# Spaced indirect transfers, a second product one step later and four buffers in a mixture-of-experts kernel

## The reference, cut to what matters

```python
x = x + 0.5 * ffn(layernorm(x))
x = x + attention(layernorm(x))      # causal, one head, within each of the 4 sequences
x = x + 0.5 * ffn(layernorm(x))

def ffn(x):                          # 8 experts, w1 128x512, w2 512x128
    probs = softmax(x @ router_w.T)
    topv, topi = top_k(probs, 2);  topv = topv / (topv.sum() + 1e-9)
    y = sum over the two chosen experts e of  topv_e * (gelu(x @ w1[e]) @ w2[e])
```

## Time and profile before

| what | value |
|---|---|
| median of 3 runs without the profiler | 332.69 us (332.57 to 332.88) |
| the profiled execution, its span | 421.0 us |
| granted TensorE clock, mean of the span | 0.850 |
| PE busy | 273.8 us |
| PE weight loads | 249.7 us |
| DVE busy | 152.5 us |
| ACT busy | 139.4 us |
| POOL busy | 140.6 us |
| indirect transfers issued by POOL | 135 |

### The profile page before, as it was taken

The page is one execution under the profiler, slowest core; times in us unless marked ns, Lnnn a source line. Parts: engine busy times, 40 slices in busy tenths (PEclk is TensorE's granted clock), DMA queues, the critical chain, the costliest instruction groups (busy, mean ns, idle before and its releaser), DMA issues.

```text
span 421.0 us, 7028 instructions
## 1 busy us (share of the span) xinstructions
PE 273.8 (65%) x1957; PEld 249.7 (59%) x1958; DVE 152.5 (36%) x687; ACT 139.4 (33%) x267; POOL 140.6 (33%) x159
## 2 busy tenths in 40 slices
PE   0505193499981599985356853699709999596930
PEld 0404183399981599963246531698709998595930
DVE  3583331222210067312497632556102222132234
ACT  1101231255540345542131412265205564243420
POOL 9047257200047200047200373000770005666550
PEclk9999996699995599998595985789866999798785
DMA  7971112522222112111000011011221222222115
GB/s 218 411 199 51 62 58 63 200 64 69 70 76 68 44 56 64 37 45 50 25 1 2 19 50 56 9 37 51 77 67 46 70 65 69 62 63 71 55 55 164
DMA packets 38520, 31.79 MB, mean 76 GB/s; under 512 B 5224, under 2 KB 34416, under 8 KB 38112
## 3 DMA queue, kind: packets, MB, share of 16 engines
q1 hardware_dynamic: 33744, 18.12, 15.2%
q0 software_dynamic: 4752, 13.40, 9.2%
HBM read 15.68 MB, written 15.81 MB: 75 GB/s over the span
## 4 chain that ended last, share of the span: by engine, by line
PE 52%; another core or an unknown queue 15%; DVE 12%; issue 11%; POOL 5%; ACT 3%; DMA 2%; DVEq 0%; POOLq 0%; ACTq 0%; SPq 0%
PE bank L890 20%; PE bank L879 19%; POOL slots_in L395 3%; PE bank L870 3%; DVE xs L707 2%; PE bank L832 2%; PE bank L847 2%; PE bank L939 2%; DVE stats L565 1%; PE bank L901 1%; DMA y_rows<-final_rows 1%; DVE xs L740 1%; DVE neg_max L731 1%; PE bank L902 1%
## 5 line engine op out<-in xcount | busy, mean ns | idle before, releaser
L890 PE MATMUL bank<-w_sb,act 128*128 x736 | 106.4, 291 | 49.5 <-issue 25.4
L890 PEld LDWEIGHTS bank<-w_sb,act 128*128 128x128 f32 x736 | 97.1, 206 | 52.0 <-issue 51.9
L879 PE MATMUL bank<-xT,w_block 128*128 128x128 f32 x736 | 108.3, 295 | 0.1
L879 PEld LDWEIGHTS bank<-xT,w_block 128*128 128x128 f32 x736 | 99.7, 210 | 0.9 <-issue 0.5
L468 ACT ACTIVATE act<-bank 128x512 f32<-128x512 f32 x92 | 54.9, 597 | 133.8 <-PE bank L879 68.9
L693 DVE COPY yb<-bank 128x128 f32<-128x128 f32 x92 | 26.7, 291 | 178.7 <-PE bank L890 109.7
L407 POOL DMA_INDIRECT y_rows<-slots_out,slot_of x48 | 46.0, 957 | 101.5 <-DMA slots_out<-yb 87.5
L462 ACT COPY w_block<-w_sb 128x512 f32 x92 | 56.4, 614 | 20.0 <-issue 20.0
L395 POOL DMA_INDIRECT slots_in<-xn,slot_of x32 | 30.9, 966 | 58.9 <-DVE slot_of L641 49.7
L418 POOL DMA_INDIRECT final_rows<-yb,row_of x23 | 22.8, 989 | 51.5 <-DVE row_of L683 38.7
L870 PE MATMUL bank<-ident,xb_numbered 128*128 128x128 f32 x92 | 28.2, 307 | 17.9 <-DMA xb_numbered<-slots_in 10.5
(11 more groups left out here) (104 smaller groups left out, 221.1 us busy)
## 6 DMA issues: line engine op xcount, KB each, us to landing
xb_numbered<-slots_in SPq DMA_DIRECT2D x69, 64.0 KB
slots_out<-yb SPq DMA_DIRECT2D x69, 64.0 KB
w_sb<-in_L_ffn_w SPq DMA_DIRECT2D x8, 512.0 KB, 8.1
slots_in<-zeros POOLq DMA_DIRECT2D x2, 1472.0 KB, 12.0
numbered_slots<-numbered POOLq DMA_DIRECT2D x1, 1483.5 KB, 5.5
xb_numbered<-numbered_slots SPq DMA_DIRECT2D x23, 64.5 KB
xs<-in_L_attn_x SPq DMA_DIRECT2D x4, 256.0 KB, 3.5
out<-xs SPq DMA_DIRECT2D x8, 128.0 KB
```

The lines of the kernel that those rows point to most:

```text
L879: mm = nc.tensor.matmul(h_ps[k][:, q * P:(q + 1) * P], w1_block[k][:, q * P:(q + 1) * P], xT[c2 % UNROLL][:], start=True, stop=True)
L890: mm = nc.tensor.matmul(y_ps[k][:, 0:D], act[k][:, q * P:(q + 1) * P], w2_sb[:, bass.ds(at + q * D, D)], start=(q == 0), stop=(q == HC - 1))
```

## The change

The second product goes from step s-3 to s-4. The copied weights and the activations get four buffers in place of two. Three of the six bursts of 16 indirect transfers get a wait in front of each transfer on the number of transposed blocks copied: transfer n (0 to 15) of `scatter(1)` waits for n+1 blocks, of `gather(0)` for 28+n, of `scatter(3)` for 47+n. DVE's `combine` of group 0 moves to steps 33, 37, 41 and 45, and the normalisation behind it with it: its pieces now begin at step 49, the last one of the phase. `HEAD`, `MIDDLE` and `LONG_HEAD` follow from `LAG` and become 11, 7 and 19 (7, 3 and 15 before): more steps are written out and fewer are in loops.

```diff
-LAG = 3
+LAG = 4
...
-        w1_block = [sb(f"w1_block{k}", [P, H]) for k in range(2)]
-        act = [sb(f"act{k}", [P, H]) for k in range(2)]
+        w1_block = [sb(f"w1_block{k}", [P, H]) for k in range(UNROLL)]
+        act = [sb(f"act{k}", [P, H]) for k in range(UNROLL)]
...
-        FIRST_COMBINE = MAX_BLOCKS + LAG + UNROLL
+        FIRST_COMBINE = MAX_BLOCKS + LAG + 6
...
-            def scatter(r):
+            def scatter(r, pace_from=None):
...
                 for t in range(GT):
                     for k in range(TOP):
+                        if pace_from is not None:
+                            pool.wait_ge(xT_copied, pace_from + TOP * t + k + 1)
...
-            def gather(p):
+            def gather(p, pace_from=None):
...
                 for t in range(GT):
                     for k in range(TOP):
+                        if pace_from is not None:
+                            pool.wait_ge(xT_copied, pace_from + TOP * t + k + 1)
...
             scatter(0)
-            scatter(1)
+            scatter(1, pace_from=0)
...
-            for p in range(GROUPS):
-                for _ in gather(p):
-                    pass
+            for _ in gather(0, pace_from=MAX_BLOCKS + LAG):
+                pass
+            for _ in gather(1):
+                pass
             scatter(2)
...
-            scatter(3)
+            scatter(3, pace_from=BLOCKS)
...
-                    G, k = nth(c - 1, i), (c - 1) % 2
-                    if c - 1 >= 2:
-                        sc.wait_ge(h_ready, G - 1)
+                    G, k = nth(c - 1, i), (c - 1) % UNROLL
+                    if c - 1 >= UNROLL:
+                        sc.wait_ge(h_ready, G - UNROLL + 1)
...
-                    if c - 2 >= 2:
-                        sc.wait_ge(y_ready, G - 1)
-                    nc.scalar.activation(act[k][:], h_ps[k][:], ACT.Gelu).then_inc(act_ready, 1)
+                    if c - 2 >= UNROLL:
+                        sc.wait_ge(y_ready, G - UNROLL + 1)
+                    nc.scalar.activation(act[k][:], h_ps[(c - 2) % 2][:], ACT.Gelu).then_inc(act_ready, 1)
...
-                q, odd = divmod(s - FIRST_COMBINE, 2)
+                q, r = divmod(s - FIRST_COMBINE, 4)
...
-                elif q >= 0 and odd:
+                elif q >= 0 and r == 0:
                     combine_and_count(0, pair_of(q))
...
-                    if 3 in stages:
-                        c3 = c - 3
+                    if LAG in stages:
+                        c3 = c - LAG
```

More of the change, by code:

```diff
@@ L458, in expert_step @@
                 if 1 in stages:
-                    G, k = nth(c - 1, i), (c - 1) % 2
-                    if c - 1 >= 2:
-                        sc.wait_ge(h_ready, G - 1)
+                    G, k = nth(c - 1, i), (c - 1) % UNROLL
+                    if c - 1 >= UNROLL:
+                        sc.wait_ge(h_ready, G - UNROLL + 1)
                     nc.scalar.copy(w1_block[k][:], w1_sb[:, bass.ds(offset[s - 1], H)]).then_inc(w1_copied, 1)
                 if 2 in stages:
-                    G, k = nth(c - 2, i), (c - 2) % 2
+                    G, k = nth(c - 2, i), (c - 2) % UNROLL
                     sc.wait_ge(h_ready, G + 1)
-                    if c - 2 >= 2:
-                        sc.wait_ge(y_ready, G - 1)
-                    nc.scalar.activation(act[k][:], h_ps[k][:], ACT.Gelu).then_inc(act_ready, 1)
+                    if c - 2 >= UNROLL:
+                        sc.wait_ge(y_ready, G - UNROLL + 1)
+                    nc.scalar.activation(act[k][:], h_ps[(c - 2) % 2][:], ACT.Gelu).then_inc(act_ready, 1)
             def expert_phase(m, **beside):
@@ L878, in step @@
                         for q in range(HC):
-                            mm = nc.tensor.matmul(h_ps[k][:, q * P:(q + 1) * P], w1_block[k][:, q * P:(q + 1) * P],
+                            mm = nc.tensor.matmul(h_ps[k][:, q * P:(q + 1) * P],
+                                                  w1_block[c2 % UNROLL][:, q * P:(q + 1) * P],
                                                   xT[c2 % UNROLL][:], start=True, stop=True)
                         mm.then_inc(h_ready, 1)
-                    if 3 in stages:
-                        c3 = c - 3
+                    if LAG in stages:
+                        c3 = c - LAG
                         G, k = nth(c3, i), c3 % 2
-                        at = offset[s - 3]
+                        at = offset[s - LAG]
                         pe.wait_ge(act_ready, G + 1)
@@ L889, in step @@
                         for q in range(HC):
-                            mm = nc.tensor.matmul(y_ps[k][:, 0:D], act[k][:, q * P:(q + 1) * P],
+                            mm = nc.tensor.matmul(y_ps[k][:, 0:D], act[c3 % UNROLL][:, q * P:(q + 1) * P],
                                                   w2_sb[:, bass.ds(at + q * D, D)], start=(q == 0), stop=(q == HC - 1))
```

## The result

The changed kernel takes 334.72 us (median of 9) against 332.69 us (9 runs of the kernel before beside it): ratio 1.0055, 95% interval 1.0034 to 1.0077, so slower by 0.55% or 1.8 us. Forecast were slower and 336.7 us. The direction is right and the time lies in the stated range, but the forecast change was 4.0 us and the measured one is 1.8.

What follows compares the result with a forecast made beforehand. Plain runs were taken as bounded by PE in the phases, POOL's queue in the last group and dependent chains elsewhere. Terms -1.0 + 3.2 + 0.8 + 1.0 = +4.0 us gave 336.7 us, range 330.0 to 339.5.

Steps and rivals of the forecast that it cites:

- the plain runs have no stalls: Whole kernel: 90 us over the undisturbed pitch in the profiled 421.0 us, leaving 331 beside a measured 332.69; chance 0.58.
- plain runs have part of the stalls: Rival, bursts and other stalled places: plain runs keep up to 12 us of stalls, so about 330.2 us; chance 0.25.
- The rule that I set against the change: Bursts: the skill says a DMA never contends with a compute engine, so spacing is worth nothing in any execution.
- +3.2 us: Seam after phase 1: the normalisation, no longer covered, delays the copy that starts attention to 4.25 us, before 1.04.
- +0.8 us: First projections after the seam: PE stands over 3 us, so one pair runs at 1.93 us in place of 1.13.
- two such pairs: First projections after the seam: upper bound of the clock's cost, two pairs at the half clock, 1.6 us.
- dearer seam: Rival, attention's start: the half clock lasts through all six projections, +2.4 in place of 0.8, 338.3 us; chance 0.07.
- LAG 4. Per step the same work ... 0 us in the PE-bound steps: Expert phases: a later second product changes nothing, since y's slack on its gelu was positive already; 0 us.
- my +1.0: Last group: POOL's chain starts later, as PE does one more transpose and h before block 69's y; bounds 0 and 1.9.
- PE ran both kinds at one pitch: 0: PE's steps in the expert phases: more written-out steps and fewer looped ones cost nothing, 0 us.
- POOL's next item, the numbered slots, is not needed before phase 2: 0: POOL's queue behind `scatter(1)`: delaying the numbered slots' transfer by spacing that burst costs nothing, 0 us.
- the wait for `gather(0)`, -1.0: End of phase 1: DVE waits some 2.3 us for the 16th transfer in the old order; gain between 0 and 2.3.

Runs made afterwards that it cites:

- the second profile: The kernel before, unchanged, profiled again: ratio 0.9993 (0.9979 to 1.0006), span 330.3 us.

## Why the prediction was right and wrong

- **Right: the plain runs have no stalls.** From the profiled execution's 421 us I subtracted 90 and got 331; the second profile has 330.3. That these are so close is partly luck, since my errors cancel. From block 3 to block 45 the stall-free time is 84.9 us and not 42 x 1.90 = 79.8, while the two attention stretches held 12.8 and 10.2 us of stalls where I took 10 each, and the first groups of phase 2 held 20.1 where I took 17.0. The 5.1 us that I booked as stalls in phase 1 are the long steps of the table: block 14 and the turns. The rival "plain runs have part of the stalls" falls: PE is busy through every burst. My forecast for the profiled span after (398) falls with it, since a burst by itself doesn't bring the stalls: after the change `scatter(3)`, not held back, runs through at 1.26 us a transfer, and PE is busy for all of it. The rule that I set against the change said that spacing is worth nothing: no run here gives the spacing of a burst a worth of its own, though ACT did come late beside one large transfer (block 14).
- **Right: the spacing of `scatter(3)` doesn't bind, and of `scatter(1)` only at the end.** After the change `scatter(3)` goes in one burst, and `scatter(1)` is first held back at the eleventh transfer.
- **Right: the last group is bounded by POOL**, shown by leaving the gather out.
- **Mis-sized: the seam.** "+3.2 us" for the exposed normalisation measured 3.7 (the first projection starts 5.38 us after the last y copy, 1.68 before). "+0.8 us" for the clock measured 2.0 in the profile after the change: the half level held through the queries' and the keys' projection of the first four tiles and into their V products, and the full level was back for the other four. That is between my "two such pairs" (1.6) and the "dearer seam" through all six projections (2.4). It is the slowest execution of nine; the same bare gap of 5.4 us between the last y copy and the first projection cost 1.35 us at the clock with `gather(0)` a burst and 0.6 with the late combine alone. The chain of waits after the change (lines 908, 909 and 914 are the first four tiles' queries, keys and V, the last row the next queries), where the earlier trace rows had 1.13:

```profile
148.58 1.71 PE bank L908 x2
150.29 1.71 PE bank L909 x2
152.00 1.22 PE bank L914 x8
153.21 0.86 PE bank L908 x2
```

- **Wrong: "LAG 4. Per step the same work ... 0 us in the PE-bound steps".** This is the step that failed. I read the slack of one step, found y in no need of more, and took that for all steps. The second loop loses 0.5 to 0.6 us at each turn, and LAG 4 hides it: phase 1 takes 95.7 us with it alone, 1.4 us less. In time it is -1.5 us where I had +1.0. "PE ran both kinds at one pitch: 0" is the same error: written-out steps and the first loop run at one pitch, the second loop does not. For the last group my +1.0 did come (its first y copy came 1.5 us later after the same h), but the steps to blocks 47, 48 and 52 became 1.6 us shorter together, so the first groups took 54.3 us (54.8 before) and not more.
- **Wrong: "POOL's next item, the numbered slots, is not needed before phase 2: 0".** Nobody waits for it, but it was in the way of ACT's turn. So the "0 us" for spacing `scatter(1)` measured -0.9.
- **Too large: the wait for `gather(0)`, -1.0.** It measured 0 at LAG 3, where DVE doesn't wait for the last pair: the step to block 40 is 2.42 with the old order and 2.40 with the late one. At LAG 4 the late order is worth some 0.4 us there (2.30 and 1.91).

So the 3.4 us that came back in phase 1 are 1.4 from LAG 4 (97.1 to 95.7), and 2.0 from the rest: 1.6 at blocks 13 to 17, where `scatter(1)` is spaced, and 0.4 at block 40. At LAG 3 spacing `scatter(1)` alone shortens the phase by 2.0 (97.1 to 95.1).

The measured parts (each against the kernel before): late combine +5.5, LAG 4 -1.5, `scatter(1)` spaced -0.9. They add up to +3.1; the whole change measured +1.8. Each of the four has an interval of 0.4 to 0.8 us to either side, so the 1.3 us between them can be noise in large part; 0.4 is block 40, and the rest stays open.

## What to carry to other kernels

Before explaining a profile, compare its span with the plain time; where they differ by a quarter, profile again before costing anything on the stalls. Read the step pitch in every loop and at every turn, not in one good stretch: one step more between a producer and its consumer can hide what a jump costs the sequencer. When work is moved out from under a loop, count the clock that the consumer loses while it waits, and look at what else on the same queue moves. And before a difference between two profiles is given a cause, see how far two profiles of the same code differ in that stretch.

## What was not expected of the hardware

- A jump back cost PE 0.5 to 0.6 us in one loop and nothing in another of the same body, and with a 1.48 MB transfer under way a copy on ACT came after 3.3 us of "issue". Both ways of moving that transfer away removed the stop, so the transfer is its cause; through what it delays ACT no run shows.
- The clock makes executions of the same code differ by about 1 us in attention. The granted clock fell to the half level at 172.0 us and came back at 185.6 in the kernel before, profiled again (the PEclk column, 1.00 and 0.50 being 2.4 and 1.2 GHz; a mixed second is split between them):

```profile
172.00:173.00 1.00, 0.00 (x0) 0.00 (x0) 1.00 (x6) 0.00 (x0) 0.00 (x0) 0.50 0.00 0
...
185.00:186.00 1.00, 1.00 (x3) 0.51 (x2) 0.86 (x5) 0.00 (x0) 0.00 (x0) 0.68 0.00 0
```

In the kernel without the last gather, whose code is the same up to there, it was 174.4 to 188.1, though the first projection of attention 1 began at 184.1 us in both:

```profile
174.00:175.00 1.00, 0.00 (x0) 0.00 (x0) 0.85 (x5) 0.00 (x0) 0.00 (x0) 0.70 0.00 0
...
188.00:189.00 1.00, 1.00 (x21) 1.00 (x19) 0.54 (x3) 0.00 (x0) 0.00 (x0) 0.97 0.00 0
```

So more of attention 1's first projections met the half level. The same happened with the numbered transfer late (173.4 to 187.1) and with LAG 4 alone. The chain of waits, first of the kernel before (profiled again), then with LAG 4 alone:

```profile
184.29 1.71 PE bank L901 x2
185.99 0.86 PE bank L902 x2
```

```profile
183.15 1.93 PE bank L908 x2
185.08 1.71 PE bank L909 x2
```

That is 1.1 us for the same four matmuls, more than the size of several terms above. Whether moving work ahead of attention makes the dearer case more likely, one profile each can't say.
